# Where q and k are rotated, where one chunk's rows are made, and who multiplies the last tile's numbers, in a fused attention and expert layer

## The reference, cut to what matters

```python
# attention, 16 heads of 8
q, k, v = split(x @ w_qkv.T)
q, k = rope(rms_norm(q, q_norm_w), rms_norm(k, k_norm_w))
att = softmax(causal(q @ k.T * 8 ** -0.5)) @ v
x = layernorm(x + att @ w_proj.T)
# experts, 8 heads, keys 32 x 32 = 1024 experts
xn = rmsnorm(x, norm_w)
s1, i1 = top_k(sim1(xn), 8)          # of 32, per row and head
s2, i2 = top_k(sim2(xn), 8)
fs, pk = top_k(s1[..., None] + s2[..., None, :], 8)
fi = (i1 * 32 + i2) at pk            # eight expert numbers per head
hidden = gelu(xn . expert_down[fi]) * relu(fs)
x = layernorm(x + sum(hidden * expert_up[fi]))
```

## Time and profile before

| what | us |
|---|---|
| median of three runs | 1596.99 (1593.52 to 1597.36) |
| the profiled execution: its time | 1597.08 |
| its span, first to last instruction | 1595.20 |
| outside the span | 1.88 |
| VectorE busy | 1370.8 (86%) |
| TensorE busy | 1352.8 (85%) |
| ScalarE busy | 910.9 (57%) |
| GpSimd busy | 663.8 (42%) |

### The profile page before, as it was taken

How to read it: one execution, slowest core, us unless ns; L and a number is a source line. 1 busy time by engine, 2 the same in 40 slices (tenths; PEclk the granted TensorE clock), 3 DMA queues, 4 the chain that set the end, 5 groups by cost and what they waited for, 6 DMA issues and landing times.

```text
span 1595.2 us, 55196 instructions
## 1 busy us (share of the span) xinstructions
PE 1352.8 (85%) x21008; PEld 975.3 (61%) x21008; DVE 1370.8 (86%) x6598; ACT 910.9 (57%) x1486; POOL 663.8 (42%) x1024
## 2 busy tenths in 40 slices
PE   5676879899898989989898989989898988987577
PEld 4343457576566757666666747666675756665557
DVE  5337799989999989989999998989999998798985
ACT  3656757565666667566666657666666756442110
POOL 3307172552708163462708264461717254050410
PEclk7787989999999989999898989989898989988667
DMA  3000000000000000000000000000000000000000
GB/s 87 7 8 8 8 9 9 15 3 9 16 9 16 9 15 9 16 2 9 16 9 16 9 15 9 10 8 9 16 9 16 3 15 3 2 16 1 9 2 17
DMA packets 30004, 18.80 MB, mean 12 GB/s; under 512 B 1840, under 2 KB 29232, under 8 KB 29744
## 3 DMA queue, kind: packets, MB, share of 16 engines
q1 hardware_dynamic: 29744, 15.23, 3.3%
HBM read 11.04 MB, written 4.19 MB: 10 GB/s over the span
## 4 chain that ended last, share of the span: by engine, by line
PE 40%; DVE 37%; issue 8%; ACT 7%; POOL 6%; DVEq 0%; ACTq 0%; POOLq 0%
DVE onehot L1278 10%; PE G L934 7%; PE F L879 7%; PE OV L823 7%; DVE topi L1224 6%; PE G L923 5%; DVE psel L1240 4%; DVE topv L1218 3%; ACT prob L644 3%; DVE whot L1303 3%; PE S L809 3%; DVE fsel L1235 2%; DVE hid L1316 2%; PE S L748 2%; POOL qk_u L455 1%
## 5 line engine op out<-in xcount | busy, mean ns | idle before, releaser
L644 ACT ACTIVATE prob<-S 128x512 f32<-128x512 f32 x640 | 371.0, 595 | 148.6 <-PE S L811 142.0
L923 PE MATMUL G<-whot,onehot 128*128 128x16 bf16 x12288 | 383.3, 171 | 30.5 <-DVE hid L1316 19.2
L923 PEld LDWEIGHTS G<-whot,onehot 128*128 128x128 bf16 x12288 | 364.5, 97 | 64.5 <-issue 16.5
L1278 DVE TENSOR_TENSOR onehot<-lo_no,elo 128x1024 bf16<-128x1024 uint16 x512 | 385.7, 802 | 0.0
L823 PE MATMUL OV<-prob,vp 128*9 128x512 f32 (+3 forms) x2048 | 183.7, 508 | 68.3 <-ACT prob L644 62.0
L508 POOL TENSOR_TENSOR gat<-gat,cande 128x1280 f16<-128x1280 f16 x64 | 178.5, 2789 | 76.6 <-DVE gat L1246 76.6
L811 PE MATMUL S<-causal,ident_b 128*128 128x128 bf16 x1024 | 201.4, 229 | 0.0
L809 PE MATMUL S<-qT,kT_even 128*128 128x512 bf16 (+3 forms) x512 | 147.1, 316 | 55.0 <-ACT prob L644 46.9
L517 POOL COPY y<-y_new 128x512 f32<-128x512 f32 x16 | 9.8, 610 | 433.9 <-DVE r L1186 378.0
L573 ACT ACTIVATE hid<-F 128x512 f32<-128x512 f32 x128 | 76.5, 597 | 185.1 <-PE F L879 185.1
L823 PEld LDWEIGHTS OV<-prob,vp 128*9 128x9 f32 x2048 | 55.2, 100 | 197.1 <-issue 106.2
(11 more groups left out here) (144 smaller groups left out, 2515.8 us busy)
## 6 DMA issues: line engine op xcount, KB each, us to landing
xa<-in_L_attn_x SPq DMA_DIRECT2D x16, 256.0 KB, 2.8
xr<-in_L_attn_x SPq DMA_DIRECT2D x16, 256.0 KB, 2.8
out<-r SPq DMA_DIRECT2D x15, 256.0 KB, 2.3
onehot<-in_L_ffn_expert_down SPq DMA_DIRECT2D x1, 512.0 KB, 5.4
up<-in_L_ffn_expert_up SPq DMA_DIRECT2D x1, 512.0 KB, 7.2
onehot<-in_L_ffn_keys SPq DMA_DIRECT2D x1, 256.0 KB, 4.5
out<-r SPq DMA_DIRECT2D x2, 128.0 KB, 1.8
onehot<-in_L_attn_w_qkv SPq DMA_DIRECT2D x1, 192.0 KB, 3.1
```

Source lines behind the costliest of these rows:

```text
L644: act.activation(dst, src, ACT.Exp, scale=SCALE).then_inc(exp_done.sem, 1)
L923: last = nc.tensor.matmul(bank[:, 16 * i:16 * i + 16], onehot[:, row, :], whot[:, t, w_part, :], start=(w_part == 0), stop=(w_part == 2))
L1278: return dve.tensor_tensor(onehot[:, row:row + 8, :].rearrange("p t (c i) -> p t c i", i=2), lo, e, ALU.is_equal)
```

## The change

Four things move and one changes engine. (a) GpSimd rotates the first half of q and k as soon as VectorE has the second quarter's weighted one-hots (`hot_done(older, 2)`) instead of after the first norm, ahead of `keep_rows`, and the second half when the first chunk has been applied (`g_free(older, 1)`), ahead of the candidates of tile 0. VectorE normalises the first half right after the first norm, the second half before the pairs of tile 0. (b) ScalarE splits the second half at step 20 instead of 17 and the rests at 23 and 24 instead of 20 and 21; GpSimd puts `gather(late, 1)` before `third_parts`. (c) VectorE makes the rows of chunk 6 (one-hots 24 to 27) and the fourth quarter's weighted one-hots after the pairs of tile 2, where they stood before and after the keys of tile 3, and applies chunk 5 after the pairs of tile 3 instead of before. (d) The multiplication of the last tile's one-hot by its candidates' numbers is VectorE's, with a semaphore of its own. (e) Within a step TensorE turns numbers and the selection right after the scores instead of near the step's end.

```diff
@@ -252,7 +252,8 @@
         fsel_done = signal("fsel_done", NT)
         top2_done = signal("top2_done", NT)
         hotc_done = signal("hotc_done", NT)
-        gat_done = signal("gat_done", NT)
+        gat_done = signal("gat_done", NT - 1)
+        last_gat_done = signal("last_gat_done", 1)
         numbers_turned = signal("numbers_turned", NT)
         hid_done = signal("hid_done", NHI, 2)
         dec = signal("dec", 4, 4)
@@ -518,18 +519,20 @@
 
             def iteration(late, older, nxt):
 
+                if nxt is not None:
+                    if older is not None:
+
+                        pool.wait_ge(hot_done.sem, hot_done.value(older, 2))
+                    rotate(nxt, 0)
                 if older is not None:
                     keep_rows(older)
-                if late is not None:
-
-                    pool.wait_ge(yi_done.sem, yi_done.value(late, 1))
                 if nxt is not None:
-                    rotate(nxt, 0)
+                    if older is not None:
+
+                        pool.wait_ge(g_free.sem, g_free.value(older, 1))
+                    rotate(nxt, 1)
                 if late is not None:
                     candidates(late, 0)
-                if nxt is not None:
-                    rotate(nxt, 1)
-                if late is not None:
                     candidates(late, 1)
                     gather(late, 0)
                 if nxt is not None:
@@ -537,14 +540,13 @@
                     rests(nxt, 1)
                 if late is not None:
                     candidates(late, 2)
+                    gather(late, 1)
                 if nxt is not None:
                     third_parts(nxt, 0)
                     third_parts(nxt, 1)
                 if late is not None:
-                    gather(late, 1)
                     candidates(late, 3)
                     gather(late, 2)
-                    gather(late, 3)
 
             iteration(None, None, 0)
             iteration(None, None, 1)
@@ -690,14 +692,14 @@
                         normed(late)
                     if late is not None and n in (8, 9):
                         similarities(late, n - 8)
-                    if nxt is not None and n in (13, 17):
-                        first_parts(nxt, (n - 13) // 4)
+                    if nxt is not None and n in (13, 20):
+                        first_parts(nxt, (n - 13) // 7)
                     if n == 12 and late is not None:
                         norm1_rows(late)
                     if n == 13 and oldest is not None:
                         norm2_rows(oldest)
-                    if nxt is not None and n in (20, 21):
-                        second_parts(nxt, n - 20)
+                    if nxt is not None and n in (23, 24):
+                        second_parts(nxt, n - 23)
                     if late is not None and n in (14, 17):
                         similarities(late, 2 + (n - 14) // 3)
                     if nxt is not None and n in QK_STEPS:
@@ -882,7 +884,10 @@
             def turn_numbers(b, t):
 
                 rows = slice(t % 2 * 64, t % 2 * 64 + 64)
-                pe.wait_ge(gat_done.sem, gat_done.value(b, t + 1))
+                if t < NT - 1:
+                    pe.wait_ge(gat_done.sem, gat_done.value(b, t + 1))
+                else:
+                    pe.wait_ge(last_gat_done.sem, last_gat_done.value(b, 1))
                 if t == 0:
                     pe.wait_ge(sims_done.sem, sims_done.value(b, 3))
                 for c in range(NCAND):
@@ -966,6 +971,10 @@
                             expert_outputs(oldest, range(2, NT))
                         if older is not None:
                             hidden_products(older)
+                    if late is not None and step in NUMBER_STEPS:
+                        turn_numbers(late, NUMBER_STEPS.index(step))
+                    if late is not None and step == SELECTION_STEP:
+                        transpose_selection(late)
                     if nxt is not None and step in QK_STEPS:
                         transpose_stack(nxt, QK_STEPS.index(step), b)
                     if older is not None and step in WEIGHT_STEPS:
@@ -979,10 +988,6 @@
                         transpose_o(b, g - 1)
                     if late is not None and step in SIMS_STEPS:
                         project_similarities(late, SIMS_STEPS.index(step))
-                    if late is not None and step in NUMBER_STEPS:
-                        turn_numbers(late, NUMBER_STEPS.index(step))
-                    if late is not None and step == SELECTION_STEP:
-                        transpose_selection(late)
                     if b is not None and u == UNITS - 1 and g < NG - 1:
                         attend(b, g)
                 if nxt is not None and shifted:
@@ -1246,6 +1251,14 @@
                 dve.tensor_tensor(gat[:, t % 2], psel[:, t % 2].unsqueeze(1).to_broadcast(dims),
                                   cand_no[:, :, :].unsqueeze(2).to_broadcast(dims), ALU.is_equal)\
                     .then_inc(hotc_done.sem, 1)
+
+            def last_gather(b):
+
+                dve.wait_ge(hotc_done.sem, hotc_done.value(b, NT))
+                t = (NT - 1) % 2
+                dve.tensor_tensor(gat[:, t], gat[:, t], cande[:, t].rearrange("p h c -> p c h").unsqueeze(3)
+                                  .to_broadcast([P, NCAND, H, TOPK]), ALU.mult)\
+                    .then_inc(last_gat_done.sem, 1)
 
             def decode(b):
 
@@ -1351,25 +1364,24 @@
                     norm1(late)
                 if oldest is not None:
                     norm2_shift(oldest)
-                one_hots(hot(20, 23))
+                if nxt is not None:
+                    normalise(nxt, 0)
+                one_hots(hot(20, 24))
                 if older is not None:
                     apply_weights(older, 0)
-                one_hots(hot(23, 24))
                 if late is not None:
                     top_keys(late, 0)
                     top_keys(late, 1)
-                if nxt is not None:
-                    normalise(nxt, 0)
                 if older is not None:
                     apply_weights(older, 1)
                 if b is not None:
                     normalise_o(b, 0)
                 if older is not None:
                     weighted_one_hots(older, 2)
+                if nxt is not None:
+                    normalise(nxt, 1)
                 if late is not None:
                     top_pairs(late, 0)
-                if nxt is not None:
-                    normalise(nxt, 1)
                 if older is not None:
                     apply_weights(older, 2)
                 if late is not None:
@@ -1377,11 +1389,8 @@
                     top_pairs(late, 1)
                 if older is not None:
                     apply_weights(older, 3)
-                one_hots(hot(24, 28))
                 if late is not None:
                     top_keys(late, 3)
-                if older is not None:
-                    weighted_one_hots(older, 3)
                 if b is not None:
                     normalise_o(b, 1)
                 if early:
@@ -1392,15 +1401,18 @@
                 if late is not None:
                     top_pairs(late, 2)
                 if older is not None:
-                    apply_weights(older, 5)
+                    one_hots(range(24, 28))
+                    weighted_one_hots(older, 3)
                 if late is not None:
                     top_pairs(late, 3)
+                    last_gather(late)
                 if b is not None:
                     normalise_o(b, 2)
                 if early:
                     keys_taken(nxt, 2)
                     keys_taken(nxt, 3)
                 if older is not None:
+                    apply_weights(older, 5)
                     one_hots(range(28, 31))
                     one_hot(31).then_inc(rows_done.sem, 1)
                     apply_weights(older, 6)
```

## The result

The changed kernel takes 1631.3 us (1631.3 to 1632.4) against 1597.2 us before: a ratio of 1.0225, interval 1.0208 to 1.0241. It is slower by 2.2%, and the forecast was 1565 us. Busy times moved as planned (GpSimd 664 to 588 us, VectorE 1371 to 1362), and yet the span grew by 34 us, to 1629.5.

What follows compares the result with a forecast made beforehand. No engine alone was the bound: VectorE and TensorE chains together. A period 2.2 us shorter, thirteen times, 28.6, plus 5 at the end less 1.5 at the start: 32.1 off 1597.08, 1565 us; range 1548 to 1590.

Steps and rivals of the forecast that it cites:

- (a): Rotation and normalisation: two root instructions hit by GpSimd's rotation, 0.9 us; TensorE's 2.29 and 2.81 us waits mostly go.
- (b): Splits and third parts on GpSimd: TensorE's first stack at A+31.4, 2.8 us earlier, with TensorE now waiting there.
- (c): VectorE's one-hots 24 to 27: 1.46 us saved from third parts, 2.41 lost beside gather 2, 0.3 for last candidates.
- (d): Last multiplication: GpSimd's gather goes, saving 2.14 us; VectorE's product takes 1.49 (nearest instruction 0.842), plus 0.1 for its semaphore.
- (e): Numbers and selection of tile 3 before the stack and part 28: VectorE's 1.86 us wait for the selection goes.
- Sum: Per period: VectorE's chain 87.4 us, TensorE's 87.3; with 1.0 for the clock 88.4, 2.2 less than before.
- the slower one: Rival, 7%: GpSimd's candidates 2, gather 1 and third parts end after A+34.2, delaying TensorE's first stack; 1614 us.
- Both must hold: In the sum: VectorE's and TensorE's chains meet within 0.3 us, so the period needs both.
- The clock: TensorE's wait before the first stack brings the lower clock behind it: a third of 3.1 us, 1.0 a period.
- The ends: Outside the thirteen full periods: 5 us gained in the last two with maxima, 1.5 lost at the start.

Runs made afterwards that it cites:

- slot 0: The changed kernel, and as a control the kernel before, each with TensorE's loop head at slot 0: 1581.8 us and 1589.5 us.
- e5: Changed kernel with TensorE's loop head at slot 0 and GpSimd's third parts ahead of gather 1: 1563.9 us, 0.9797 of the kernel before.
- experiment 2: Kernel before with three semaphore-raising instructions added at the end of TensorE's loop body: 1646.3 us, 1.0320 of the kernel before.
- slot 104: Kernel before, nothing added, with TensorE's loop head at slot 104: 1641.4 us, one run.

## Why the prediction was wrong

The step that failed is the **Sum**: "TensorE: part 24 stood at A+44.27 ... From there 46.34 us less some 0.5 of small waits: 87.3." It takes the time of the loop's end over unchanged. I counted (d)'s new semaphore at 0.1 us on VectorE (the trace has 0.5 us of idle time ahead of all sixteen products) and not at all on TensorE, where its wait value adds three register instructions a turn; they moved the closing branch, for 3.2 us at the branch and 1.3 or 2.1 of lower clock behind it in each of 11 turns; these turns are 51 us longer than at slot 0. No rival had it: the slower one was GpSimd as the gate at step 27, and the first stack was on time. Nothing in the rows that I read shows that the branch stood within three instructions of a dear place. It could have been bounded by a test of its place, or by the exit, at which the kernel before already stood still for 3.81 us.

The same term was wrong without the branch. At slot 0 part 24 stands at A+41.9 (A at 929.6; A+41.5 forecast, A+42.5 with the clock's 1.0), but from there to the next A it is 46.8 us, not 45.8. The wait of 0.84 us for ScalarE's copy, which (e) brought, is in it.

At equal placement the change saves 7.7 us by the medians (1589.5 to 1581.8) and 15.2 in the traces, of which the one before is the slowest of its six runs and the one after the fastest of its four; I had 32.1. Point by point:

- **(a)** Right, and over-priced: 0 us instead of 0.9. GpSimd's timeline in the changed kernel shows the rotation of half 0 over, with all six instructions undisturbed, 1.1 us ahead of the root's first instruction at 668.83:

```profile
663.47 0.73 POOL L456 TENSOR_TENSOR gat<-qk_r,cosw 128x256 f32<-128x256 f32 x1 [39.77 <-DVE whot L1316]
...
667.01 0.73 POOL L461 TENSOR_TENSOR qk_r<-gat,qk_u 128x256 f32<-128x256 f32 x1
```

  In the loop ScalarE's waits for q and k and TensorE's 2.29 and 2.81 are gone; 1.00 and 0.69 us remain.
- **(b)** Right: forecast A+31.4, measured A+30.8, with the wait that I named. That third parts ahead of the gather would do better I did not see; that order is 18 us faster, about half of it by the four slow turns that it hasn't.
- **(c)** The gather's cost was right: the three weighted one-hots take 4.18 us beside it for 2.04 undisturbed, and the four one-hots ahead of them 2.77 for 2.49, 2.4 us together. But it was called a loss of 1.25 us a period on VectorE, and taking it back loses 2.2 (89.97 to 92.19): the sum had left out what the one-hots do to candidates 2.
- **(d)** The product measured 1.49 us as forecast:

```profile
L1259 DVE TENSOR_TENSOR gat<-gat,cande 128x1280 f16<-128x1280 f16 x16 | 23.9, 1492 | 0.5
```

  Of my two values the larger held, 1.49 us against the 0.84 of the earlier trace rows; which difference of the two instructions makes it so no run shows. The gather's hold-up of one-hots 28 to 31 is gone too (2.49 us), and the whole is worth 2 us or nothing: it was not on the path.
- **(e)** Wrong in the loop. The wait was removed at the decode and came back at three later places, because TensorE sets the time from the v-projection on; and TensorE has the wait of 0.84 us more. "Both must hold" was true of the sum and not used for this step.
- **The clock.** Right as far as it went: behind the first stack the clock is at 0.50 (961.50:964.00 above), and from the stack to the third group it is 6.3 us (960.39 to 966.65) where it was 5.3 (785.20 to 790.49), the 1.0 that I had put in. But it also fell over the second group in four turns of eleven, each 2.3 us longer than the others' mean: 0.85 us a period that I did not have. The earlier trace rows had shown the low clock there, and I took it to go with the two stalls.
- **The ends.** Two of the thirteen full periods lie ahead of the first closing branch, so I had 2 x 2.2 - 1.5 = 2.9 us gained there; 0.5 were lost. Behind the loop 10 were gained (forecast 5).

What was left of 2.2 us a period is 0.5 in the mean (90.48 to 89.97) and 1.4 in the seven turns without a slow second group, 89.1 in the mean. e5 comes to 1.7 and, with the same end, to within 1 us of the forecast time; but the forecast was for another order, and this agreement is luck and supports none of its steps.

## What to carry to other kernels

Three instructions more inside a hardware loop moved the loop's closing branch here, and with it the price of each turn, from 0.36 to 3.45 us in the median (experiment 2). So before and after are to be compared with the loop's head pinned to the same slot, at more than one slot (the changed kernel took 1581.8 us at 0, 1583.4 at 92 and 1597.5 at 224), and the branch's own duration read first, with the idle time behind it. A wait that ends on one engine is gained only if the next thing that engine needs is not set by the same late partner. And where two engines hold each other up, both lists are to be followed: the one with slack in busy time can be the gate of the other.

## What the runs showed of the hardware

- A taken back edge of TensorE cost 0.36 or 0.45 us in the median, or 3.2 to 3.9, by the place of the code alone (2.3 and 3.1 in two turns at slot 104); one more instruction packet of 16.4 KB a turn went with the places that stall (12 for 11). The group of 32 matmuls behind a dear one took 3.6 or 4.46 us for 2.34 in the changed kernel; one of 3.62 lay in a stretch with a mean granted clock of 0.67 (741.00:745.00), one of 4.46 in one with 0.50 (834.50:838.90).
- The exit of the same loop, a branch that is not taken, stalled TensorE for 3.81 us in the kernel before and not at slot 0.
- With the loop's head at slot 224 the branch was cheap (0.45 us in the median) and a stall of 1.35 us stood in the work behind it; the period was 91.6 us for 90.0 at slot 0.
- In one kernel the granted clock fell to 0.50 in four of eleven turns behind the same instructions and the same waits.
- GpSimd's ten instructions for one tile's candidates took 4.9 us beside VectorE's 1024-column one-hots (without (c), 881.14 to 886.06) and 3.1 where those stand elsewhere (the change at slot 0, 952.09 to 955.16); single ones of 0.24 to 0.30 us took 0.69 to 0.79.
- Sixteen transposes of the stack (128x128 bf16) took 1.89 us at a granted clock of 0.50 (changed kernel, 711.14, 711.20:712.90) and eight took 0.61 us at 1.00 (kernel before, 785.20:785.80). From start to start it is 107 and 56 ns in the median of the kernel before (L759), that is 1.2 and 2.3 columns a ns. That is what the runs show of the levels that the prediction calls 1.2 and 2.4 GHz.
